# Two layers with adaptive norms, 32 x 256 tokens: the mixing stage rewritten with tokens on partitions

## The reference, cut to what matters

```python
# o: output of the delta rule, [B, L, 16 heads, 8]
o = o * rsqrt(mean(o * o, axis=-1) + 1e-6) * rms_w        # norm 1: over the 8 channels of a head
x = x + ga * (o.reshape(B, L, 128) @ Wout.T + bout)
h = layernorm(x) * (1 + cb) + sb                          # norm 2: over 128 channels, then scale and shift per batch
# the expert layer gets h, and its skip is h:
xn = h * norm_scale * rsqrt(mean(h * h, axis=-1) + 1e-6)  # norm 3: over 128 channels
scores = xn @ w_router.T                                  # 8 scores
ids = top_k(scores, 2); c = softmax(scores)[ids]
val, gate = split(xn @ w_up[e].T)                         # for each chosen expert e
y = (val * silu(gate)) @ w_down[e].T
x = x + gb * (h + sum(c * y))
```

## Time and profile before

| | us |
|---|---|
| median of 3 runs | 2906.77 (2906.42 to 2907.79) |
| the profiled execution, its time | 2903.59 |
| its span, first to last instruction | 2901.8 |
| mix stage, from its first DMA issue to ffn's first instruction | 2202.8 to 2533.2 |
| busy in the span: PE, DVE, ACT, POOL | 2130.3, 2081.0, 1252.2, 1395.3 |
| mean granted TensorE clock | 0.845 of 2.4 GHz |

### The profile page before, as it was taken

How to read it: one execution, slowest core, us unless ns; L and a number is a source line. 1 busy time by engine, 2 the same in 40 slices (tenths; PEclk the granted TensorE clock), 3 DMA queues, 4 the chain that set the end, 5 groups by cost and what they waited for, 6 DMA issues and landing times. The chain is left out here.

```text
span 2901.8 us, 43350 instructions
## 1 busy us (share of the span) xinstructions
PE 2130.3 (73%) x12242; PEld 1738.9 (60%) x12242; DVE 2081.0 (72%) x6516; ACT 1252.2 (43%) x2935; POOL 1395.3 (48%) x1249
## 2 busy tenths in 40 slices
PE   4688888898888856745466637888884656299994
PEld 4578787787877733323345426677763323199993
DVE  6677777777787779962388887778784888455556
ACT  3534444344443412211266616667772222155551
POOL 2344454544445312147346556888883355444440
PEclk8799999999999967765577769999997766599995
DMA  2000000000000030012311000000003011122216
GB/s 92 15 1 1 1 1 1 1 1 1 1 1 1 1 138 19 21 52 42 71 44 44 30 0 1 1 1 1 1 1 128 23 33 34 42 68 66 65 53 177
DMA packets 103387, 92.62 MB, mean 32 GB/s; under 512 B 11824, under 2 KB 93872, under 8 KB 102448
## 3 DMA queue, kind: packets, MB, share of 16 engines
q1 hardware_dynamic: 80112, 63.36, 7.1%
q0 software_dynamic: 14592, 22.30, 3.0%
q10 hardware_dynamic: 8448, 4.20, 0.5%
HBM read 46.84 MB, written 42.98 MB: 31 GB/s over the span
## 5 line engine op out<-in xcount | busy, mean ns | idle before, releaser
L658 PE MATMUL attn_out<-attn_turned,attn_v_diag 128*128 128x256 f32 (+7 forms) x2048 | 304.8, 305 | 23.5 <-DVE attn_turned L828 23.5
L658 PEld LDWEIGHTS attn_out<-attn_turned,attn_v_diag 128*128 128x128 f32 x2048 | 300.2, 191 | 35.9 <-issue 26.1
L716 ACT ACTIVATE attn_p_att<-attn_score,attn_mx 128x224 f32<-128x224 f32 (+7 forms) x512 | 149.1, 391 | 385.4 <-DVE attn_mx L806 385.4
L2185 POOL TENSOR_TENSOR delta_A<-delta_A,delta_sW 128x256 f32<-128x256 f32 x256 | 186.1, 727 | 93.1 <-ACT delta_sW L2065 68.1
L2002 PE MATMUL delta_u<-delta_v_own,tables_sb 128*128 128x256 f32 x512 | 159.0, 393 | 77.3 <-ACT delta_v_own L2054 77.3
L2699 POOL DMA_INDIRECT choice_rows<-ffn_y,ffn_xg x136 | 130.4, 959 | 173.7 <-DVE ffn_y L2806 168.9
L647 PE MATMUL attn_score<-attn_k,attn_q_diag 128*128 128x256 f32 (+3 forms) x1024 | 211.7, 348 | 2.3 <-ACT attn_p_att L716 2.3
L2131 DVE TENSOR_TENSOR delta_u<-delta_u,xT 128x256 f32<-128x256 f32 x256 | 153.6, 600 | 78.7 <-PE delta_u L2006 71.8
L2065 ACT ACTIVATE delta_sW<-delta_W,tables_sb 128x256 f32<-128x256 f32 x256 | 128.7, 503 | 140.3 <-issue 119.0
L2194 POOL TENSOR_TENSOR delta_m<-delta_A,qT 128x1024 f32<-128x1024 f32 x64 | 183.8, 2873 | 5.0
L704 ACT ACTIVATE attn_p_geo<-attn_kp_wide,attn_geo_cols 128x32 f32<-128x32 f32 (+6 forms) x448 | 180.1, 518 | 0.0
(11 more groups left out here) (371 smaller groups left out, 5727.3 us busy)
## 6 DMA issues: line engine op xcount, KB each, us to landing
ffn_xg<-rows SPq DMA_DIRECT2D x136, 66.0 KB
acc<-route_zero SPq DMA_DIRECT2D x10, 832.0 KB
proj_rows<-acc SPq DMA_DIRECT2D x32, 256.0 KB, 4.4
comb_rows<-choice_rows SPq DMA_DIRECT2D x32, 256.0 KB
rows<-route_rows SPq DMA_DIRECT2D x16, 320.0 KB, 3.6
load_rows<-in_x SPq DMA_DIRECT2D x16, 256.0 KB
x_kept<-xT SPq DMA_DIRECT2D x16, 256.0 KB, 2.1
xT<-x_kept SPq DMA_DIRECT2D x1, 4096.0 KB, 12.2
```

What stands on the lines that cost most here:

```text
L658: last = nc.tensor.matmul(O[kind][:, gr * T + SLOT * n:(gr + 1) * T], v_diag[:, gr * KB + n], turned[:, kind, gr, n * T + SLOT * n:(n + 1) ...
L716: last = nc.scalar.activation(p_att[:, gr, ROW_OFF[n]:ROW_OFF[n + 1]], score[at][:, c:c + SLOT * (n + 1)], ACT.Exp, bias=mx[:, gr, n:n + 1])
L2185: nc.gpsimd.tensor_tensor(A[:, t % 8], A[:, (t - 1) % 8], sW[:, t % 4], ALU.add).then_inc(k.A, 1)
```

## The change

Only `mix_phase` is changed. The pair of chunks (8 tiles of 128 tokens, `SIDE`) is handled as one unit, and the statistics of all three norms have tokens on partitions:

- Norm 1: PE multiplies with the squares as weights, 8 times 16 columns (`sum_heads`), which gives 16 sums for each token. After the roots PE turns the 128 columns (`narrow`), ACT copies them, and 8 products with selecting matrices (`pick`, made by POOL at the start) spread them to channels (`widen`). DVE multiplies (`scale_heads`).
- Norm 2: PE turns the residual to rows (`back`), DVE takes mean and variance with bn_stats and bn_aggr (`statistics`), ACT norms each tile with scale and bias per token (`norm`), and PE turns back (`channels`).
- Norm 3: PE sums the squares with 8 products of one column (`sum_rows`). The root isn't applied to h. It is applied to the 64 scores on DVE and, by ACT, to the rows when they are copied out, one tile at a time (`copy_rows`).
- One run of Newton steps (`roots`) serves the heads of iteration b+1, norm 2 of iteration b and norm 3 of iteration b-1, over 144 columns.
- norm_scale is put into the router's weights by DVE and into w_up by ACT (`scale_up`, 4 pieces of 1408 columns).
- The ranks come from 9 products with shifted slices of one mask, in place of 28. POOL sends a pair at a time.
- The first 1024 tokens of the residual are loaded by a DMA of their own, and the loading of w_up comes before w_down. PE no longer waits for the residual at the start.

The diff, cut to its core:

```diff
+    SIDE = PAR * TILES
+    RMS, NORM, HEAD = slice(0, SIDE), slice(SIDE, 2 * SIDE), slice(2 * SIDE, 2 * SIDE + SIDE * HEADS)
...
-            sp.dma_start(g.keptT[:, :], g.x_kept).then_inc(c.x_in, 16)
+            sp.dma_start(g.keptT[:, 0:PAR * CH], g.x_kept[:, 0:PAR * CH]).then_inc(c.x_first, 16)
+            sp.dma_start(g.keptT[:, PAR * CH:N], g.x_kept[:, PAR * CH:N]).then_inc(c.x_rest, 16)
...
-            pe.wait_ge(c.x_in, 16)
...
+            def sum_heads(i):
...
+                    pe.wait_ge(k[par].sq0, i + 1)
+                    for r in range(TILES):
+                        first = par * TILES + r
+                        last = nc.tensor.matmul(head_sums[:, first:first + 128 - SIDE + 1:SIDE], sq[:, 0, par, 128 * r:128 * r + 128],
+                                                g.t("same_head")[:, 0:128:DH1], start=True, stop=True)
+            def narrow(i):
+                pe.wait_ge(c.newton, ROOT * (i + 1))
...
+                nc.tensor.transpose(narrow_ps, root_y[:, i % 2, HEAD], g.t("ident")).then_inc(c.narrow, 1)
+            def widen(i):
+                pe.wait_ge(c.narrow_out, i + 1)
...
+                        last = nc.tensor.matmul(mid[par][:, 128 * r:128 * r + 128], pick[:, par * TILES + r, :], inv_t[:, :],
+            def router_and_rows(i):
+                if i > 0:
+                    pe.wait_ge(c.counted, i)
+                for par in both:
+                    pe.wait_ge(k[par].modulated, i + 1)
+                    if i > 0:
+                        pe.wait_ge(k[par].rows_read, i)
+                    for r in range(TILES):
...
+                        nc.tensor.transpose(rowt[par][:, 128 * r:128 * r + 128], h, g.t("ident"))
+                        last = nc.tensor.matmul(logits[:, j * E1:(j + 1) * E1], h, router[:, :], start=True, stop=True)
+            def sum_rows(i):
...
+                        last = nc.tensor.matmul(row_sums[:, j:j + 1], sq[:, 1, par, 128 * r:128 * r + 128],
+                                                g.t("ones")[:, 0:1], start=True, stop=True)
             def count(i):
...
+                nc.tensor.matmul(counts, before[:, :], flat, start=True, stop=False)
+                for d in range(1, SIDE + 1):
+                    last = nc.tensor.matmul(counts[:, d * E1:WIDTH], ones[:, :], flat[:, 0:WIDTH - d * E1],
+                                            start=False, stop=d == SIDE)
...
+            sum_heads(0)
+            for b in range(-1, LAST + 2):
+                if b + 1 <= LAST:
+                    if b == -1:
+                        pe.wait_ge(c.picks, SIDE)
+                    narrow(b + 1)
+                    widen(b + 1)
+                if 0 <= b <= LAST:
+                    channels(b)
+                if b + 1 <= LAST:
+                    project_out(b + 1)
+                if b >= 1:
+                    count(b - 1)
+                if b + 2 <= LAST:
+                    sum_heads(b + 2)
+                if 0 <= b <= LAST:
+                    router_and_rows(b)
+                if b + 1 <= LAST:
+                    back(b + 1)
+                if 0 <= b <= LAST:
+                    sum_rows(b)
...
         @block.scalar
...
+            head_squares(1)
+            for b in range(-1, LAST + 2):
+                if b + 1 <= LAST:
+                    narrow(b + 1)
+                if 0 <= b <= LAST:
+                    norm(b)
+                if b + 1 <= LAST:
+                    add_bias(b + 1)
+                if 0 <= b <= LAST:
+                    modulate(b)
+                    square(b)
+                if b >= 1:
+                    exps(b - 1)
+                    copy_rows(b - 1)
+                if 0 <= b < PIECES:
+                    scale_up(b)
+                if 2 <= b + 3 <= LAST:
+                    head_squares(b + 3)
...
         @block.vector
...
+            for b in range(-1, LAST + 2):
+                roots(b + 1, b + 1 if b + 1 <= LAST else None, b if 0 <= b <= LAST else None, b - 1 if b >= 1 else None)
+                then = choose(b - 1) if b >= 1 else None
+                if b + 1 <= LAST:
+                    scale_heads(b + 1)
+                if b >= 1:
+                    rank(b - 1)
+                if b == LAST + 1:
+                    tile_table()
+                if b + 1 <= LAST:
+                    add_mixed(b + 1)
+                if b >= 1:
+                    share(b - 1, then)
+                if 0 <= b <= LAST:
+                    skip(b)
+                if b + 1 <= LAST:
+                    statistics(b + 1)
```

More of the change, by code:

```diff
@@ new lines, in mix_phase @@
+        top_at = s.sb("top_at", [128, SIDE, 8], U32)
+        onehot = s.sb("onehot", [128, SIDE, K1, E1])
+        mask = s.sb("mask", [128, SIDE + 1, E1], BF16)
+        less = s.sb("less", [128, SIDE, E1])
+        ex = s.sb("ex", [128, SIDE, E1])
+        total = s.sb("total", [128, SIDE])
+        place = s.sb("place", [128, SIDE, E1])
+        own = s.sb("own", [128, SIDE, K1, E1])
+        place_of = s.sb("place_of", [128, SIDE, K1])
+        base = s.sb("base", [128, E1])
+        mid = [s.ps(f"mid{par}") for par in range(PAR)]
@@ new lines, in mix_phase @@
+        front = [s.ps(f"front{par}") for par in range(PAR)]
+        rowt = [s.ps(f"rowt{par}") for par in range(PAR)]
+        small = s.ps("small")
+        sums = s.ps("sums")
+        head_sums, narrow_ps = sums[:, 0:128], sums[:, 128:256]
+        row_sums, logits, counts = small[:, 0:SIDE], small[:, 8:8 + SIDE * E1], small[:, 72:72 + (SIDE + 1) * E1]
+        c = s.sems("w_in w_ready x_first x_rest up_in up_scaled down_in consts picks region filled spare_in fills_in table ids_made"
+                   " heads heads_read row_sums sums_read norm_v guess newton shift stats moments narrow narrow_out"
+                   " logits scored route mask placed counted owned ranked exp named slots")
@@ L2412, in copy_out, with scale_up @@
                     last.then_inc(k[par].rows_read, 1)
             def exps(i):
[L2415 to L2418 removed]
+                act.wait_ge(c.route, ROUTE * i + SIDE + 1)
+                nc.scalar.activation(ex[:, :, :], less[:, :, :], ACT.Exp).then_inc(c.exp, 1)
+            def scale_up(n):
+                if n == 0:
+                    act.wait_ge(c.up_in, 16)
+                some = g.w_up[:, n * (2 * E1 // PIECES):(n + 1) * (2 * E1 // PIECES), :]
+                nc.scalar.activation(some, some, ACT.Copy, scale=per_channel[:, 2:3]).then_inc(c.up_scaled, 1)
@@ new lines, in choose @@
+                dve.wait_ge(c.scored, i + 1)
+                nc.vector.tensor_copy(seen[:, 0:1], score[:, 0, 0:1])
+                for j in range(SIDE):
+                    then(nc.vector.max(top[:, j, :], score[:, j, :]), wait=False)
+                then.done()
+                if i > 0:
+                    dve.wait_ge(c.exp, i)
+                then(nc.vector.tensor_tensor(less[:, :, :], top[:, :, :], top[:, :, 0:1].to_broadcast([128, SIDE, E1]), ALU.subtract),
+                     wait=False)
```

503 lines of the change are left out of this document (229 added, 274 removed).

## The result

The change was timed in three further sets of runs, each beside the kernel before on the same chip.

| runs of the change | change | before | ratio, 95% interval |
|---|---|---|---|
| first measurement (chip not recorded) | 2891.0 | 2906.6 | 0.9944 (0.993 to 0.9958) |
| `after_again`, chip 13 | 2893.3 | 2909.4 | 0.9946 (0.9929 to 0.9963) |
| `after_fourth`, chip 9 | 2891.4 | 2910.3 | 0.9938 (0.9915 to 0.9962) |
| `after_third`, chip 15 | 2843.2 | 2903.2 | 0.9794 (0.9777 to 0.981) |

The account below looks back on a forecast made before the run. The chain through all engines, no longer DVE, was taken to bound the stage, at 25.7 us a pass against 36. POOL's last issue: 2263 + 5 x 25.7 + 2 x 22.1 + 20.6 = 2456.3, 71.2 us earlier, so 2836, range 2815 to 2866.

Parts of the forecast that it names:

- The last three terms: End of the stage, bound by POOL: sends 7 and 8 start 22.1 us after one another, the last takes 20.6.
- The row at 1.94 us: A slow POOL issue at 2326.88 against a median of 0.958, for which a send was costed at 22.1 us.
- The estimate of 21.0: An iteration's sends on POOL by the skill's reading, in place of 22.1; the sum would be 2 us less.
- Steps 1 to 4: One pass from the roots' start: roots 4.0, widen done 8.7, project_out 11.8, modulate 14.7, ACT's row copies 19.95 us.
- Step 5: Router on PE after the rows are read: 2.7 us at the low clock, then 1.9 for the second half, ending 22.6.
- Step 6: End of a pass: back 1.0, sum_rows 1.9 at the high clock, hops 0.3; next roots start at 25.7 us.
- Step 3: channels and project_out on PE, 1.2 and 1.9 us with the clock rising at 9, ending at 11.8; norms and choosing ready.
- The clock stays low: Rival: PE's low clock lasts, pass 31.7 us, first send 11 us later, 2877; chance of passes above 27.5 us 0.18.
- POOL is the bound: Rival: the pass falls to 22.1 us and DVE waits for slots in rank, 2818; chance of passes below 24 us 0.16.
- Slower: Rival: small PE products pay weight load and product one after the other, pass 43 us, kernel 2957; chance 0.03.
- No change: Rival: pass near 36 us by another way, or a stage end not set by POOL; chance 0.01.
- The signs that I named: Profile signs: roots every 25 to 26 us, steps near 0.29, L2359 waiting some 3.5 for L2475, POOL waiting before sends 2 to 6.

Follow-up runs that it names:

- warm_pe: The change plus dummy PE products of 256 columns in two idle stretches, 6 before the router, 12 after sum_rows; 2830.6 us, 0.9747 of before.
- warm_pe_again: The same file as warm_pe (the change plus dummy PE products), run once more on chip 15; 2830.6 us, 0.9757 of before.
- warm_roots: The change with only the 12 dummy PE products after sum_rows, none ahead of the router, on chip 13; 2899.8 us, 0.9967 of before.

## Why the prediction was right in direction and wrong in size

**The sum, against the chip without stalls.** The last issue was forecast to end at 2456.3; in `after_third` it ends at 2467.4. Of these 11.1 us, 4.6 are the stage's start (SP's first DMA at 2207.3 instead of 2202.8, earlier stages that the change does not touch), 1.1 the first send, and 5.4 the pass: five gaps of 26.8 us on average (25.85 to 27.25) against 25.7. The last three terms (2 x 22.1 + 20.6) came to 64.9 against 64.8, by luck: they were 21.3, 22.1 and 21.4. A send of an iteration was costed at 22.1 and took 20.3 (2294.52 to 2314.8, where the copy behind it ends); POOL waits in the first five passes, so that cost nothing there. The row at 1.94 us had made me too high. The estimate of 21.0 by the Trainium skill, "SBUF — State Buffer", section "Who interferes with whom", was nearer, though no run here shows that its reason is the right one.

**The pass, step by step** (times after the roots' start, from the rows of `after_third`). Steps 1 to 4: the turn starts at 4.2 (forecast 4.0), `widen` takes 3.78 (3.8), `project_out` ends at 12.15 (11.8), modulate at 14.7 (14.7). ACT's row copies take 3.04 us, not 3.85. Step 5: the router is done, and `back` starts, at 21.75 (22.6), its second half at the low clock, where I had put a rise. **Step 6 failed**: `back` was put at 1.0 and `sum_rows` at 1.9, "at the high level", and they took 1.95 and 3.41, at 1.2 GHz; with the hops 5.3 us against 3.1 (the terms 1.0, 1.9 and 0.3 make 3.2; the sum went on with 25.7). The 2.2 us lost there, less the 0.9 that the router was early, make the +1.3 of this pass. The rule that I cited from the Trainium skill, "TensorE: Matmul & The Clock Gate", section "HAM oscillation — how this bites in real kernels", that bursts between waits are throttled anew, agrees with this trace: 3.31 us idle, then 0.50 through the whole burst.

**The 16 us of the first measurement.** Its terms against the forecast: start of the stage +4.1, first send +3.1, five gaps of 33.5 to 34.7 in place of 25.7 +40.6, the last three terms +11.6, together 59.4 us. The step that failed is again step 6, in its words "DVE's statistics end at the same moment" and "0.3 for hops": I took it that DVE starts when its semaphores are there. On chips 9 and 13, and in the first measurement, it does not. Step 3 failed by the same, in "choosing on DVE are ready by then": the stall before `less` holds up `scale_heads` behind it, and `project_out` starts 11.3 to 13.4 us after the roots' start, not at 9.9. Once it then found PE at the low clock:

```profile
2295.10 3.78 PE L2329 MATMUL mix_mid<-mix_on,mix_w_out 128*128 128x512 f32 x4 [3.71 <-DVE mix_on L2572]
```

Over the five passes between the roots at 2281.72 and at 2452.32 a pass took 34.1 us on average, 8.4 more than 25.7: `back` starts at 24.05 (22.6 to 26.8), +1.5; `back` and `sum_rows` at the low clock, +2.0; and the stall from the end of L2370 to L2531, 4.2 to 5.6 us and 4.9 on average.

**The rivals.** "The clock stays low" came near the time (2877) with a wrong mechanism: low from step 3 on it was not (`project_out`, L2329, took 1.88 us in the pass shown of `after_third` and 1.98 in four passes of the first measurement; the 3.78 above is the exception). "POOL is the bound", "Slower" and "No change" did not occur; the products and weight loads overlapped as forecast (16 records of L2370 in 3.41 us at the low clock). No rival had DVE held up by sends. The signs that I named held in part: steps at 0.31 us, not 0.29; L2359 waits 3.3 us for L2475; POOL waits before sends 2 to 6 and, in `after_third`, hardly before the last two (6.5 and 5.1 us in the first measurement). The roots start 26.9 to 27.1 us apart from the third pass of `after_third` on, and 31.9 to 37.5 in the first measurement, not 25 to 26.

**What stays open**: why chips 9 and 13 stall and 1, 8, 11 and 15 do not; what of the sends DVE and ACT wait for there. Part of the stall lies behind POOL's last issue, so it may be the landing of the rows and not POOL's work, or a supply of instructions that the sends slow down; no run separates these. Open too: why the kernel before, with 76 DVE records beside one send of 22.6 us (2340.6 to 2363.2), shows hardly a stall in the middle of its stage, where the change has 41 in 20.0 us in the first measurement (63 in 20.1 us in `after_third`), and whether its profile came from a stalling chip. `warm_pe` is the fastest version (ratio to before 0.975 to 0.976 on chips 1, 8 and 15, and 12.6 us faster than the change on chip 15). It was not run on a stalling chip; on chip 13 its halves were 6 to 9 us slower than the change, so it cannot be recommended for all chips.

## What to carry to other kernels

When a chain through all engines replaces a busy engine, read every gap between a semaphore's last producer and its consumer: a wait whose releaser the profile cannot name is a cost of its own, and such rows may already stand in the profile of before. Price a burst on PE by the idle time ahead of it; 3.3 us of idle time cost this pass 2.4 us in its last two groups (1.95 and 3.41 us against 1.07 and 1.84 in `warm_pe_again`). And if one chip's result misses a sum whose steps all hold, run the same file on another chip before changing the theory.

## What the runs showed of the hardware that I had not expected

- One file takes 2843 us on chip 15 and 2891 to 2893 us on chips 9 and 13, while the kernel before differs by 7 us between them (2903.2 to 2910.3). The difference is in stalls, not in the pace of all work.
- On the stalling chips DVE's short instructions go on in steps of 0.7 and 1.4 us while POOL issues indirect DMAs 1.26 us apart; 16 plain DMAs of the same size, issued by SP in 14.1 us, do nothing of the kind.
- There a stall can outlast POOL's last issue by 2.65 to 2.90 us (first measurement), and ACT stalls too, up to 6.7 us in `warm_roots`.
- The nine steps of the roots behind the first guess, two inputs in SBUF each, ran at 0.31 us beside the sends on both sorts of chip, and POOL's issues kept their median of 0.958 us.
